# Sinkhorn stage of a fused megakernel: last two rounds written out behind the loops, the stop test ahead of the last group's turn, r and c in one load, six opening products for eight

## The reference

```
K = exp(-M / MU);  K = K / max(K.sum over a batch element, EPS)
u = r; u_prev = 1; v = 0
repeat 31 times:
    diff   = sqrt(sum((u - u_prev)^2, last axis))
    active = max(diff) > TOL
    v_new  = c / max(K^T u, EPS)
    u_new  = r / max(K v_new, EPS)
    where active: u, u_prev, v = u_new, u, v_new
P = u * K * v^T
```

## Time and profile before

| | us |
|---|---|
| runs shown, median (lowest, highest) | 496.57 (496.02, 497.24) |
| the profiled execution's own time | 496.99 |
| its span in the profile | 495.3 |
| PE busy in the span | 472.5 (95%) |
| DVE busy | 348.8 (70%) |
| ACT busy | 324.1 (65%) |

### The profile page before, as it was taken

How to read it: one execution, slowest core, us unless ns; L and a number is a source line. 1 busy time by engine, 2 the same in 40 slices (tenths; PEclk the granted TensorE clock), 3 DMA queues, 4 the chain that set the end, 5 groups by cost and what they waited for, 6 DMA issues and landing times. The chain is left out here.

```text
span 495.3 us, 24307 instructions
## 1 busy us (share of the span) xinstructions
PE 472.5 (95%) x9142; PEld 393.8 (80%) x9142; DVE 348.8 (70%) x1268; ACT 324.1 (65%) x808; POOL 234.7 (47%) x579
## 2 busy tenths in 40 slices
PE   8999999999999999999999998789999988999996
PEld 6899999999977545666666677678888877999996
DVE  6888888888877575766657656477888887734443
ACT  5455555556546963656665666577877768987773
POOL 3244444444453001055443554643477775777454
PEclk9999999999999999999999999999999999999999
DMA  5170000000000075143424000022233344555300
GB/s 177 45 257 0 0 0 0 0 0 0 0 2 2 28 162 130 42 77 85 86 54 123 1 1 2 31 63 71 64 118 111 122 139 148 167 162 153 98 30 27
DMA packets 23394, 34.42 MB, mean 69 GB/s; under 512 B 4096, under 2 KB 14341, under 8 KB 23208
## 3 DMA queue, kind: packets, MB, share of 16 engines
q1 hardware_dynamic: 20560, 27.23, 20.3%
q0 software_dynamic: 2784, 6.56, 3.7%
HBM read 23.88 MB, written 8.26 MB: 65 GB/s over the span
## 5 line engine op out<-in xcount | busy, mean ns | idle before, releaser
L206 ACT ACTIVATE den_v<-ps_g,floor 128x128 f32<-128x128 f32 x124 | 45.5, 367 | 38.9 <-PE ps_g L266 32.4
L266 PE MATMUL ps_g<-buf_a,u_pad 128*32 128x128 f32 x1984 | 66.7, 274 | 0.0
L280 PE MATMUL ps_g<-buf_b,v_pad 128*32 128x128 f32 x1984 | 63.7, 275 | 0.2
L266 PEld LDWEIGHTS ps_g<-buf_a,u_pad 128*32 128x32 f32 x1984 | 52.1, 110 | 2.6 <-issue 0.3
L280 PEld LDWEIGHTS ps_g<-buf_b,v_pad 128*32 128x32 f32 x1984 | 50.2, 109 | 1.8 <-DVE v_pad L374 0.5
L1433 POOL DMA_INDIRECT out<-buf_d,token_i x39 | 38.5, 988 | 23.8 <-DVE buf_c L1940 17.2
L374 DVE RECIPROCAL v_pad<-ps_g 128x32 f32<-128x32 f32 x124 | 38.8, 333 | 15.6 <-PE ps_g L272 13.5
L767 PE MATMUL ps_h<-buf_c,up 128*128 128x512 f32 x96 | 49.1, 607 | 0.6 <-DVE buf_c L1046 0.4
L192 POOL TENSOR_SCALAR held_u<-inv_u 128x8 f32<-128x8 f32 x124 | 23.8, 192 | 45.5 <-DVE inv_u L383 45.4
L1649 PE MATMUL ps_ss<-xT,buf_d 128*128 128x128 f32 x312 | 41.4, 276 | 0.0
L1649 PEld LDWEIGHTS ps_ss<-xT,buf_d 128*128 128x128 f32 x312 | 37.9, 192 | 0.4 <-ACT xT L1775 0.2
(11 more groups left out here) (360 smaller groups left out, 1253.3 us busy)
## 6 DMA issues: line engine op xcount, KB each, us to landing
cw_b<-cw_d SPq DMA_DIRECT2D x16, 512.0 KB, 7.6
buf_c<-sorted_x SPq DMA_DIRECT2D x39, 136.0 KB, 2.2
buf_a<-in_x SPq DMA_DIRECT2D x8, 256.0 KB, 5.2
buf_d<-in_x_nt SPq DMA_DIRECT2D x1, 2048.0 KB, 9.7
state<-buf_a SPq DMA_DIRECT2D x16, 128.0 KB, 2.0
x<-in_w SPq DMA_DIRECT2D x8, 256.0 KB, 3.1
buf_b<-in_w SPq DMA_DIRECT2D x8, 256.0 KB, 3.2
sorted_x<-nobody SPq DMA_DIRECT2D x1, 1088.0 KB, 11.0
```

The costliest lines, as they stand in the source:

```text
L206: fn(den_v[:, h, :], ps_v[h], ACT.Relu, bias=floor[:, h:h + 1]).then_inc(v_den, 1)
L266: last = mm(ps_v[h][32 * j:32 * j + 32, :], u_pad[:, h, j, 32 * i:32 * i + 32], K[:, t * D:(t + 1) * D], start=i == 0, stop=i == TI - 1)
L280: last = mm(ps_u[h][32 * c:32 * c + 32, :], v_pad[:, h, c, 32 * i:32 * i + 32], KT[:, b * N:(b + BG) * N], start=i == 0, stop=i == TI - 1)
```

## The change

- The loops of PE and DVE run 14 passes instead of 15; rounds 29 and 30 follow them written out. In round 30 DVE no longer writes u for a next round (four `spread` operations go).
- In round 30 PE sums the counts (`overs`) between `to_rows(2)` and `to_rows(3)`. PE no longer waits for `u_ready[0]` before the 14 products.
- DVE runs the stop test's chain after `inverse(2)` and before `turn_back(3)` and `inverse(3)`. The last of its four operations goes: the histories of counts get one more column that is always 0, so that the minimum never passes 31, and the reduction writes the integer itself.
- r and c are columns of one input and come in one load.
- PE opens with 6 products of the identity instead of 8.

```
-                sp.dma_start(r_t[:], io["r_t"]).then_inc(s["r_in"], 16)
-                sp.dma_start(c_t[:], io["cond_t"]).then_inc(s["c_in"], 16)
+                sp.dma_start(r_c[:], io["r_c"]).then_inc(s["r_in"], 16)
...
-                c.step(g.iota(rounds[:], pattern=[[1, ITERS]], base=0, channel_multiplier=0,
+                c.step(g.iota(rounds[:], pattern=[[1, ITERS + 1]], base=0, channel_multiplier=0,
                               allow_small_or_imprecise_dtypes=True))
                 c.step(g.memset(ones[:], 1.0))
+                c.step(g.memset(moved[:, ITERS, :], 0.0))
...
                 pe.wait_ge(s["made"], IDENT)
-                for _ in range(8):
+                for _ in range(6):
                     mm(ps_g[3][:, 0:P], ident[:], ident[:], start=True, stop=True)
...
+                def overs():
+                    pe.wait_ge(s["judged"], NG * ITERS)
+                    mm(ps_s[0:1, 0:ITERS + 1], ones[:, 0:1], moved[:, :, 0], start=True, stop=True).then_inc(s["overs"], 1)
+
-                def one_round(i):
+                def one_round(i, last=False):
...
                     for h in range(1, NG):
                         pe.wait_ge(v_ready, i + h + 1)
                         to_rows(h)
+                        if last and h == 2:
+                            overs()
...
-                with nc.tensor.Fori(NG, NG * ITERS, 2 * NG) as i:
+                with nc.tensor.Fori(NG, NG * (ITERS - 2), 2 * NG) as i:
                     one_round(i)
                     one_round(i + NG)
-                pe.wait_ge(s["judged"], NG * ITERS)
-                mm(ps_s[0:1, 0:ITERS], ones[:, 0:1], moved[:, :, 0], start=True, stop=True).then_inc(s["overs"], 1)
-                pe.wait_ge(u_ready[0], NG * (ITERS + 1))
+                one_round(NG * (ITERS - 2))
+                one_round(NG * (ITERS - 1), True)
                 for _ in range(14):
                     mm(ps_g[0][:, 0:P], ident[:], ident[:], start=True, stop=True)
...
-                with nc.vector.Fori(NG, NG * ITERS, 2 * NG) as i:
+                with nc.vector.Fori(NG, NG * (ITERS - 2), 2 * NG) as i:
                     one_round(i)
                     one_round(i + NG)
-
+                one_round(NG * (ITERS - 2))
+                i = NG * (ITERS - 1)
+                for h in range(NG - 1):
+                    invert(h, i)
+                turn_back(0, i)
+                invert(NG - 1, i)
+                inverse(0, i)
+                turn_back(1, i)
+                inverse(1, i)
+                turn_back(2, i)
+                inverse(2, i)
                 c = Chain(dve, s["kdone"])
                 dve.wait_ge(s["overs"], 1)
...
-                c.step(v.tensor_reduce(stop[:], still[:, 1, :], AX.X, ALU.min))
-                c.step(v.tensor_scalar(stop_i[:], stop[:], float(ITERS), None, ALU.min))
+                with nc.allow_low_precision(reason="whole numbers below 100"):
+                    c.step(v.tensor_reduce(stop_i[:], still[:, 1, :], AX.X, ALU.min))
+                turn_back(NG - 1, i)
+                inverse(NG - 1, i)
                 k = v.value_load(stop_i[0:1, 0:1], min_val=0, max_val=ITERS)
```

More of the change, by code:

```diff
@@ L68, in sinkhorn @@
     ABOVE = TI * BG
-    IDENT, OWN, PADDED, SIDED, READY = 2, 5, 8, 13, 21
+    IDENT, OWN, PADDED, SIDED, READY = 2, 5, 8, 13, 22
     with ExitStack() as ctx:
@@ L76, in sinkhorn @@
         ones_pad = mem.sb("ones_pad", [P, TI * WIDE])
-        rounds = mem.sb("rounds", [1, ITERS])
+        rounds = mem.sb("rounds", [1, ITERS + 1])
         pick = mem.sb("pick", [P, BG, BG, TI])
-        c_t = mem.sb("c_t", [P, B])
-        r_t = mem.sb("r_t", [P, G])
+        r_c = mem.sb("r_c", [P, G + B])
+        r_t, c_t = r_c[:, 0:G], r_c[:, G:G + B]
         ksum = mem.sb("ksum", [P, NG])
@@ L92, in sinkhorn @@
         over = mem.sb("over", [P, 2, G])
-        still = mem.sb("still", [1, 2, ITERS])
-        stop = mem.sb("stop", [1, 1])
+        still = mem.sb("still", [1, 2, ITERS + 1])
         stop_i = mem.sb("stop_i", [1, 1], I32)
-        moved = mem.sb("moved", [P, ITERS, NG])
+        moved = mem.sb("moved", [P, ITERS + 1, NG])
         ps_g = [mem.ps(f"ps_g{k}", [P, 512]) for k in range(NG)]
@@ L102, in sinkhorn @@
         ps_k = [mem.ps(f"ps_k{k}", [P, HT * P]) for k in range(KBANKS)]
-        s = {n: mem.sem("s_" + n) for n in ("made", "clear", "r_in", "c_in", "k_exp", "k_mm", "kt_done", "sums_mm", "summed",
+        s = {n: mem.sem("s_" + n) for n in ("made", "clear", "r_in", "k_exp", "k_mm", "kt_done", "sums_mm", "summed",
                                             "floors", "diffed", "u_read", "judged", "overs", "v_kept", "held", "seen", "kdone")}
@@ L352, in _ @@
                    ALU.mult).then_inc(s["clear"], 1)
-                v.tensor_copy(u_hist[:, G:2 * G], r_t[:]).then_inc(u_kept, NG)
-                dve.wait_ge(s["c_in"], 16)
+                v.tensor_copy(u_hist[:, G:2 * G], r_t).then_inc(u_kept, NG)
                 dve.wait_ge(s["made"], SIDED)
@@ L361, in scaled @@
                        ps_k[k % KBANKS][:].rearrange("p (t q n) -> p q t n", q=BG, n=N),
-                       c_t[:].rearrange("p (q t) -> p q t", q=BG)[:, :, ts, None].broadcast_to([P, BG, HT, N]),
+                       c_t.rearrange("p (q t) -> p q t", q=BG)[:, :, ts, None].broadcast_to([P, BG, HT, N]),
                        ALU.mult).then_inc(s["kt_done"], 1)
@@ L421, in _ @@
                 finish(0)
-                with nc.vector.Fori(NG, NG * ITERS, 2 * NG) as i:
+                with nc.vector.Fori(NG, NG * (ITERS - 2), 2 * NG) as i:
                     one_round(i)
                     one_round(i + NG)
+                one_round(NG * (ITERS - 2))
[9 more added lines that the diff above has]
+                inverse(2, i)
                 c = Chain(dve, s["kdone"])
                 dve.wait_ge(s["overs"], 1)
-                c.step(v.tensor_scalar(still[:, 0, :], ps_s[0:1, 0:ITERS], 0.0, float(2 * ITERS), ALU.is_gt, ALU.mult))
+                c.step(v.tensor_scalar(still[:, 0, :], ps_s[0:1, 0:ITERS + 1], 0.0, float(2 * ITERS), ALU.is_gt, ALU.mult))
                 c.step(v.tensor_tensor(still[:, 1, :], still[:, 0, :], rounds[:], ALU.add))
-                c.step(v.tensor_reduce(stop[:], still[:, 1, :], AX.X, ALU.min))
-                c.step(v.tensor_scalar(stop_i[:], stop[:], float(ITERS), None, ALU.min))
+                with nc.allow_low_precision(reason="whole numbers below 100"):
+                    c.step(v.tensor_reduce(stop_i[:], still[:, 1, :], AX.X, ALU.min))
+                turn_back(NG - 1, i)
+                inverse(NG - 1, i)
                 k = v.value_load(stop_i[0:1, 0:1], min_val=0, max_val=ITERS)
@@ L2076 @@
         "cond_t": a["cond_1024"].T,
-        "r_t": a["fside_BxS_0"][order].reshape(G, P).T,
+        "r_c": np.concatenate([a["fside_BxS_0"][order].reshape(G, P).T, a["cond_1024"].T], 1),
         "gate_w0_t": a["L0_ffn_gate_weight"].T,
```

## The result

The changed kernel takes 498.46 us (median of 20 runs, 496.85 to 500.30); the kernel before, run beside it, 496.47 (20 runs, 496.02 to 498.68). The medians lie 2.0 us apart. The ratio of the runs is put at 1.0032, interval 1.0022 to 1.0043, which is 1.6 us slower. Both are outside the range forecast (495.0 to 497.1). The kernel before timed against itself later gave 1.0012 (0.9999 to 1.0026), so a ratio up to about 1.001 says nothing here. The profiled execution took 499.46, against 496.99.

A forecast was written before the change was run, and what follows sets the result against it. Bounds: loads at the start, a relay with PE pausing little in the rounds, a DVE-PE tie at the end. Terms 0.35 + 0 + 0.12 + 0.08 = 0.55 us gave 496.02 us, range 495.0 to 497.1.

The forecast's parts named there:

- The gain before the barrier: Start, loops and stage end together: 0.55 us won before 143.0 us and carried to the kernel's end.
- the load's 0.35 us: Start: one load for r and c lets later pieces of x begin earlier; 0.35 us won, bounds 0 and 0.47.
- The branch's 0.12: Loop's branch back between rounds 28 and 29 goes, the step falling from 4.11 to 3.99 us: 0.12 us won.
- the bound of 0.41: Written-out rounds: a first pass through new code may cost 0.41 us, leaving 0.29 lost; as a rival, chance 0.13.
- the premise that the fifth piece sets when the rounds begin: Start: PE waits at 10.36 us for ACT's exponential of x's fifth piece, so its earlier arrival starts the rounds earlier.
- The six products' zero: Start: 0.94 us of PE work saved by two fewer opening products is spent waiting for x's second piece; 0 won.
- the sign named for it: Start: PE would be back at the upper clock level before the second piece's transposes at 5.8 us.
- The chain: Stage end: DVE through 0.65 us earlier, but PE's unread products then hold the barrier, so only 0.08 us won.

The follow-up runs named there:

- c1_after: The changed kernel again, unaltered, as the yardstick for the follow-up experiments: ratio to the kernel before 1.0033.
- e1_end: The kernel before with only the end's edits (two rounds out of the loops, sum and chain ahead of the last group): ratio 1.0036.
- e3_open8: The changed kernel with eight opening products again instead of six: ratio to the kernel before 1.0029.
- e6_peel: The kernel before with rounds 29 and 30 written out on both PE and DVE, nothing else: ratio 1.0045.
- e7_peel_pe: The kernel before with rounds 29 and 30 written out on PE alone, DVE's loop kept: ratio 1.0031.
- e8_peel_dve: The kernel before with rounds 29 and 30 written out on DVE alone, PE's loop kept: ratio 1.0005.
- e13_dve_out: The kernel before with DVE's rounds written out, short chain behind the last group, PE's loop kept without the `u_ready` wait, 10 closing products: 496.49 us, ratio 0.9989.

## Why the prediction was wrong

**The step that failed** is the first paragraph's: "What comes behind starts at the barrier and has the same instructions, so whatever is won or lost before 143.0 us should be carried to the end as it is." They are the same instructions at other places in PE's code. PE's instructions come in 16 KB packets by DMA; two written-out rounds moved the fetches behind the barrier by about half their spacing, and they meet other work there. The ratios sort by PE's written-out rounds: the six kernels with two rounds of PE written out (the changed one, `c1_after`, `e1_end`, `e3_open8`, `e6_peel`, `e7_peel_pe`) have 1.0029 to 1.0045; the nine that keep PE's loop have 0.9989 to 1.0020; the three with four rounds out 1.0013 to 1.0022. The intervals of neighbours overlap; what carries the reading are the kernels timed on one chip side by side (`e6_peel` and `e7_peel_pe` against `e8_peel_dve`). Among runs with a mean granted clock above 0.997 the medians are 497.8 us (five kernels with two rounds out, 36 runs), 497.5 (four rounds, 22), 497.0 (loop kept, 74, the one of before against itself among them) and 496.7 (before, 122). So PE's written-out code is shown as the cause; that it acts through the places of the fetches is shown in profiles for a part, and argued for the rest.

The gain before the barrier failed as well: 0.55 us was forecast, and the next stage's first product came 0.31 us later than in before in the changed kernel's profile and 0.16 us earlier in that of `c1_after`. In the first the load's 0.35 us is missing (below). In the second the rounds began 0.60 us earlier, but the step from round 29 to 30 and the stretch from there to the next stage took 4.19 and 5.48 us, against 3.99 and 5.21 in before.

The Trainium skill, "Runtime: NRT & Kernel Launch", "Instruction fetch mechanics", gives blocks of 16 KiB, 256 instructions, and calls the cost of crossing one "mostly hidden". The packets of PE agree in size (29, 0.48 MB). That the cost is hidden holds for most of them here (`e7_peel_pe` has 22 of them ahead of 412 us and is 0.07 us from before there); at 411 us one stood with a scatter's last packet behind it, and there the trace decides.

**What each place costs.** Shown in profiles: 0 to 0.69 us in a written-out round; 2.65 to 4.77 us from the scatter's issue to SP's load. That was 4.33, 4.42, 4.56 and 4.77 in four of the six kernels with two rounds out, 2.65 in the other two (the fetch came at 407.91, and at 411.49, after the last packet), and 2.65 to 4.08 in all others, before itself having 3.81, with a fetch at 409.40 among the packets. So the place costs before 1.2 us too, and the changed kernel's own profile lost nothing there: it came 2.3 us late already, and met the fetch at another moment. Between 413 and 416 us the six profiles with two rounds out lose 0.37 us on average against before (-0.40 to +0.95), the other thirteen, before among them, gain 0.20 (-0.47 to +0.31). That is 0.57 us, half of what the medians differ by.

**Two rounds out of the loops.** The branch's 0.12 came as worked out (3.98 against 3.99 forecast). First passes through new code cost less than the bound of 0.41 in the changed kernel's profile (29 to 30 took 4.04 us, 0.05 more) and more than it in `e6_peel`. The term's size is not one number.

**One load, six products.** The load's 0.35 us failed, and with it the premise that the fifth piece sets when the rounds begin. The fifth piece came 0.60 us earlier (exponential at 9.08; 9.3 was forecast), but the third came late (7.79), PE did the rest without a pause from 8.47 on, and was at the fifth at 10.69 in place of 10.0. Which piece is late varies from profile to profile, and before's own profile, from which the premise was read, has the latest fifth piece of the thirteen with two loads (9.68; the others 8.69 to 9.46). The six products' zero stands as not disproved, though the sign named for it failed: in the changed kernel's profile the level was up at 7.16 us (5.28 in before), and the transposes of the first two pieces ran at the lower one (8 records in 2.03 us).

**The chain.** Right in its order: DVE 1.0 us ahead of PE, PE's products next, nothing waited for `judged`. Its 0.08 us is not to be seen: from group 0's last transpose to the next stage it is 5.28, 5.48, 5.11 and 5.08 us in the four kernels with the change's whole end, against 5.21. What no term had is a fixed 0.32 us at 246 us, in all eight kernels that have the short chain on DVE, and in none of the other ten. After, then before:

```profile
245.69 0.32 DVE L1141 TENSOR_TENSOR ln_y<-kept,fresh 128x128 f32<-128x128 f32 x1 [0.17 <-DVE fresh L1138]
...
248.44 0.49 PE L903 MATMUL ps_gc<-rh,gru_wh 128*128 128x128 f32 x2 [0.77 <-DVE rh L1133]
```

```profile
245.24 0.29 DVE L1126 TENSOR_TENSOR ln_y<-kept,fresh 128x128 f32<-128x128 f32 x1
...
247.80 0.49 PE L888 MATMUL ps_gc<-rh,gru_wh 128*128 128x128 f32 x2 [0.45 <-DVE rh L1118]
```

DVE pauses between two of its own instructions, and PE then waits 0.32 us longer for it; a fetch of 8 KB of instructions that are not PE's follows 0.7 us later, at 246.4 us, where before has none. That it is a block end in DVE's code is argued, not shown, since `e6_peel` and `e8_peel_dve` have such a fetch at the same place and no pause.

**Still open.** Where the other half of the 1.1 us between medians goes, since each kernel has one profile; and whether four rounds out really cost less than two. Why TensorE's level drops for a moment late in some executions (328.0 to 331.4 us here, 1.56 us; also from 325.9, 327.1, 328.5 and 417.2 in other kernels, 1.3 to 1.6 us each): a granted clock of 0.997 or less was seen in 21% of before's runs, 40% of the runs of the five other kernels with two rounds out (34% with the changed kernel's), 39% with four and 30% with the loop kept, too near each other over so few runs to blame the code.

## What to carry to other kernels

Adding code to one engine moves every later instruction block of that engine; here, with the engine 95% busy and DMA-fed stages behind, a change that was to win 0.1 to 0.5 us lost more there than it could win. Try writing loops out on the engine with slack first, and leave the busy engine's code length alone (`e13_dve_out` did so, and is the only kernel with a ratio below 1). Don't read which load bounds a start from one profile: the late piece was another one in the next. Time the kernel against itself before reading ratios of 0.1%: a forecast of "no change" needs a bound for what moves behind the change, not only for the change.

## What the runs showed of the hardware

- An instruction fetch of 16 KB took 0.88 to 2.32 us over the 19 profiles. In four of them a scatter's last packet began within 0.02 us of a fetch's end: 4.33 to 4.77 us to the next load in place of 2.65.
- With c's 512 bytes a partition in r's load, one issue less, the pieces of x were issued 0.47 us earlier, and yet ACT waited up to 2.4 us for one of them, not the same one in each kernel's profile.
- TensorE's upper level came between 4.8 and 11.1 us from one kernel's profile to the next, late (10.6 to 11.1) with six and with eight opening products; the three late ones put the rounds' start 1.3 to 1.6 us behind before's.
